# A graph-attention block on one core: for 6 of 16 source tiles ScalarE writes turned masks into the score banks, TensorE adds the scores; the first and the last stage are ordered anew

## The chip, the cores and the metric

The kernel runs on one core of one Trainium2 chip. The metric is the device time in microseconds (us) of one execution, the median of several. The engines are named PE (TensorE), DVE (VectorE), ACT (ScalarE), POOL (GpSimd) and SP (SyncE, which here only issues DMAs).

## The reference

One graph-attention layer with 2048 sources, 2048 targets, width 256, 8 heads of 32. Cut to what matters:

```python
h  = relu(layernorm(x));  hs = layer_norm(h) * s1 + b1;  ht = layer_norm(h_target) * s1 + b1
q, k, v = (ht @ Wq + bq) / sqrt(32), hs @ Wk + bk, hs @ Wv + bv
logits  = where(adj != 0, einsum('thd,shd->hts', q, k), -1e30)
ctx     = einsum('hts,shd->thd', softmax(logits), v)
ht      = layer_norm(ht + ctx @ Wo + bo) * s2 + b2
out     = x + ht + gelu(ht @ W1) @ W2
```

Everything is float32 in and out. The kernel splits most operands into a 16-bit high part and a 16-bit rest.

## The kernel before, in words

Targets are taken in 4 blocks (`NTB`) of 512, and in each block the 8 heads one after another: 32 *units* (`UNITS`), unit u being block k = u // 8 and head r = u % 8. A unit has 16 *steps* (`STEPS`), one for each tile of 128 sources; n = 16 u + step numbers them all, to 512.

A step n needs a tile of masked, shifted scores. `scores(n)` on PE writes it into one of two banks, `score[n % 2]`: four matmuls of 128 columns lay minus the mask, turned by the negative identity `nidentb` (`mask_nat` holds 1e30 where there is no edge, targets on the partitions), and one of 512 columns adds the scores. ACT takes the exponential into `prob` (`exponential(n)`), POOL or DVE makes its low part `prob_lo` (`low_part(n)`; DVE has steps 2, 6, 10 and 14 of most units), and `context(n)` on PE adds 8 matmuls of 65 columns to the bank `ctx`. PE issues `scores` five steps (`AHEAD`) before `context`; `scores(n)` waits for `exponential(n - 2)`, since the bank must be free.

The shift of a unit is the maximum of its scores, found ahead of time: `early_scores` (PE, 512 columns, two to a pair) and `maxima` (DVE, 1024 elements, with the mask) work on 8 pairs per unit, 14 pairs (`LEAD`) ahead, in two buffers `early`. So each pair on PE waits for the maxima of the pair two before. The maxima go through `shift_row` (PE), `negated` and `row_out` (ACT) into the query rows. One bank, `aux`, serves all small jobs one after another (`aux_job`, `AUX`): shift rows, turned contexts (`cT`), the output product (`wo`), turned targets (`qT`), query projections (`qp`). Tables such as `CT_AT` or `MASK_DVE` give (head, step) or (head, pair) of each; every engine runs its own list in order, with semaphores between them. ACT copies the context bank out once per unit (`context_out`), at the start of the next one.

The first stage normalizes, projects keys, queries and values, and moves keys and queries by DMA into the layout of the heads (`place_k`, `place_q`: 32 partitions x 1024 elements each, 48 + 12 of them, in groups g of two heads, all from SP). `sum_values` gives the mean of the values (for targets without an edge) by 32 matmuls into `aux`. `up_bias` in unit 1 computes the bias that the second layer norm's bias gives the feed-forward product, by 32 matmuls of one column, and `scale_weight` (DVE, units 2 to 5) multiplies W1 by the norm's scale.

The last stage runs the feed-forward part per block of targets: `up_products` (PE, 6 x 512 columns for each of 8 slices f), `gelus` (ACT, the function and a copy), `gelu_low` (DVE), `down_products`; between them `turn_block`, `block_high` and `block_low` bring in the next block, and `results` (DVE) frees the row banks.

## Time and profile before

| | |
|---|---|
| median of 3 runs (lowest, highest) | 723.34 us (723.26, 723.36) |
| profiled execution: its own time, its span | 727.01 us, 725.2 us |
| PE busy | 672.5 us (93%) |
| DVE busy | 591.6 us (82%) |
| POOL busy | 517.4 us (71%) |
| ACT busy | 451.7 us (62%) |
| first exponential starts, last context copy starts | 76.62 us, 620.76 us |

Busy is the time in which an engine runs at least one instruction, over the span. Matmuls overlap in the pipeline, so a busy PE is not one at its peak. The three stages are read apart: before 76.62 us, the 32 units up to 620.76 us, and the rest.

### The profile page before, as it was taken

The numbers are of one execution on the slowest core, as the hardware profiler recorded it, in microseconds if no ns is written. First come the engines' busy times: TensorE is split into PE (matmuls) and PEld (weight loads), VectorE is DVE, ScalarE is ACT, GpSimd is POOL, SyncE is SP. The second block draws the span as 40 slices with busy tenths as digits, with TensorE's granted clock in tenths as the row PEclk, the third lists the DMA queues.
The fourth block names the chain that finished last, engine by engine and source line by source line (L and its number), as shares of the span: only waits on it lengthen the run. The fifth ranks groups of instructions, "written<-read, shape, count | busy, mean of one in ns | idle before, by whom it ended". The sixth has DMA issues, their size and how long they took to land.

```text
span 725.2 us, 20296 instructions
## 1 busy us (share of the span) xinstructions
PE 672.5 (93%) x8386; PEld 479.8 (66%) x8386; DVE 591.6 (82%) x974; ACT 451.7 (62%) x806; POOL 517.4 (71%) x494
## 2 busy tenths in 40 slices
PE   4968889899999999999999999999999899889998
PEld 4536567666677677667767776677677667556667
DVE  5947687999989997999999899989977987554651
ACT  4632446666677656877766586677666778836650
POOL 3720657979899996789999778899977777442430
PEclk9979998999999999999999999999999999989999
DMA  8373610211200111130000201103000000000001
GB/s 296 112 196 79 236 31 2 70 45 57 81 2 2 31 57 34 44 104 17 2 31 2 89 30 54 38 2 118 2 2 2 3 2 2 1 1 23 23 22 52
DMA packets 20796, 36.22 MB, mean 50 GB/s; under 512 B 2752, under 2 KB 13280, under 8 KB 20704
## 3 DMA queue, kind: packets, MB, share of 16 engines
q1 hardware_dynamic: 20704, 34.92, 15.6%
q8 instruction: 66, 1.08, 0.6%
q14 instruction: 26, 0.21, 0.1%
HBM read 26.49 MB, written 2.10 MB: 39 GB/s over the span
## 4 chain that ended last, share of the span: by engine, by line
PE 56%; DVE 30%; issue 8%; SPq 2%; ACT 2%; DMA 1%; DVEq 0%; ACTq 0%
PE score L442 24%; DVE early L1147 14%; PE early L442 14%; PE ctx L442 10%; PE aux L442 6%; DVE prob_lo L1155 6%; SPq L358 2%; DVE mask_nat L1135 1%; DVE st_x L1070 1%; DVE half_max L1147 1%; DVE q_stage L1173 1%; DMA node_i<-in_nodemask 1%; DVE st_l L1065 1%; DMA kT<-mask_nat 1%; DVE col_l L1193 0%
## 5 line engine op out<-in xcount | busy, mean ns | idle before, releaser
L1350 POOL TENSOR_TENSOR prob_lo<-prob 128x512 f16<-128x512 f32 x376 | 434.9, 1181 | 109.8 <-ACT prob L856 108.3
L856 ACT ACTIVATE prob<-score 128x512 f32<-128x512 f32 x512 | 304.8, 597 | 173.9 <-PE score L442 166.2
L442 PE MATMUL early<-kT,qT 96*128 96x512 f16 x512 | 193.3, 383 | 28.1 <-DVE half_max L1147 20.8
L442 PE MATMUL score<-nidentb,mask_nat 128*128 128x128 bf16 x2048 | 198.9, 220 | 2.6 <-ACT prob L856 1.4
L442 PE MATMUL score<-qT,kT 97*128 97x512 f16 x512 | 196.0, 383 | 0.0
L442 PEld LDWEIGHTS ctx<-v_sb,prob 128*128 128x128 bf16 x2048 | 160.0, 98 | 54.3 <-ACT raw L878 9.3
L442 PE MATMUL ctx<-v_sb,prob 128*128 128x65 f16 x2048 | 192.3, 193 | 0.6 <-POOL prob_lo L1350 0.5
L442 PE MATMUL ctx<-v_sb,prob_lo 128*128 128x65 f16 x2048 | 191.1, 193 | 0.0
L1147 DVE CUSTOM_DVE_ANT_0 early<-early,mask_nat,half_max 128x1024 f32<-128x1024 f32 x128 | 163.6, 1285 | 28.4 <-PE early L442 27.9
L1147 DVE CUSTOM_DVE_ANT_0 early<-early,mask_nat 128x1024 f32<-128x1024 f32 x128 | 156.8, 1229 | 25.6 <-PE early L442 23.7
L442 PEld LDWEIGHTS ctx<-v_sb,prob_lo 128*128 128x128 f16 x2048 | 143.4, 97 | 50.2 <-issue 4.8
L1155 DVE TENSOR_TENSOR prob_lo<-prob 128x512 f16<-128x512 f32 x136 | 137.0, 1008 | 8.9 <-ACT prob L856 8.9
L442 PEld LDWEIGHTS score<-nidentb,mask_nat 128*128 128x128 bf16 x2048 | 122.4, 98 | 5.7 <-ACT prob L856 2.6
L442 PEld LDWEIGHTS early<-kT,qT 96*128 96x128 f16 x512 | 50.4, 99 | 49.3 <-DVE half_max L1147 40.0
L1449 POOL TENSOR_TENSOR mask_nat<-mask_nat,tgt 128x256 f32<-128x256 f32 x16 | 15.3, 966 | 51.7 <-DVE mask_nat L1300 51.7
L442 PEld LDWEIGHTS score<-qT,kT 97*128 97x128 f16 x512 | 50.2, 98 | 0.0
L1286 DVE TENSOR_TENSOR kT<-qT,kT 128x512 f16<-128x512 f32 x32 | 25.3, 794 | 26.8 <-ACT kT L1026 26.8
L442 PE MATMUL early<-w_f,kT 128*128 128x256 f16 x384 | 42.6, 273 | 1.6 <-DVE adj_in L1310 1.6
L442 PEld LDWEIGHTS early<-w_f,kT 128*128 128x128 f16 x384 | 37.5, 98 | 6.9 <-DVE adj_in L1310 1.9
L1021 ACT ACTIVATE qT<-score,bias_f 128x512 f32<-128x512 f32 x32 | 21.9, 684 | 28.2 <-PE score L442 24.8
L1147 DVE DVE_READ_ACCUMULATOR2_ANT half_max<- 128x1 f32 x256 | 35.4, 138 | 0.0
L1135 DVE TENSOR_SCALAR mask_nat<-adj_in 128x1024 bf16<-128x1024 int32 x26 | 29.6, 1140 | 0.0
(167 smaller groups left out, 609.1 us busy)
## 6 DMA issues: line engine op xcount, KB each, us to landing
adj_in<-in_adj SPq DMA_DIRECT2D x26, 512.0 KB, 3.8
qT<-q_stage SPq DMA_DIRECT2D x48, 64.0 KB, 2.0
kT<-mask_nat SPq DMA_DIRECT2D x48, 64.0 KB, 2.0
raw<-in_x SPq DMA_DIRECT2D x4, 512.0 KB, 5.1
tgt<-in_L_gnn_h_target SPq DMA_DIRECT2D x4, 512.0 KB, 8.4
prob<-in_adj SPq DMA_DIRECT2D x4, 512.0 KB, 8.4
nT<-in_L_gnn_W SPq DMA_DIRECT2D x2, 1024.0 KB, 7.5
mask_nat<-in_x SPq DMA_DIRECT2D x1, 2048.0 KB, 8.3
```

The costliest lines, as they stand in the source:

```text
L358: sp.dma_start(dst[r * HD:(r + 1) * HD, 2 * g:2 * g + 2, :].rearrange("p h t -> p (h t)"), stage[g * HD:(g + 1) * HD, part, :, :].rearrang ...
L442: return nc.tensor.matmul(dst, w, m, start=start, stop=stop, **more)
L856: nc.scalar.activation(prob[:, n % SLOTS, :], score[n % 2][:, :], ACT.Exp).then_inc(exp_done, 1)
L1021: nc.scalar.activation(gelu[:, f % 2, :], up[f % 2][:, :], ACT.Gelu_apprx_tanh, bias=bias_f[:, f:f + 1]).then_inc(gelu_ready, 1)
L1065: link(nc.vector.bn_stats(dst[:, n, :], tile))
L1070: last = nc.vector.bn_stats(dst[:, first + t, :], tile(t))
L1135: nc.vector.tensor_scalar(mask_half(k, i), adj_home(k, i), 0.0, BIG, ALU.is_equal, ALU.mult).then_inc(mask_dve, 1)
L1147: nc.vector.tensor_tensor_reduce(out=early[e % 2][:, :], in0=early[e % 2][:, :], in1=mask_nat[:, k % 2, t, half * HALF:(half + 1) * HALF], ...
L1155: nc.vector.tensor_tensor(prob_lo[:, n % SLOTS, :], prob[:, n % SLOTS, :], prob_hi(n % SLOTS), ALU.subtract).then_inc(lo_sem["dve"], 1)
L1286: nc.vector.tensor_tensor(g_lo[:, k % 2, f, :], gelu[:, f % 2, :], g_hi[:, k % 2, f, :], ALU.subtract).then_inc(g_lo_done, 1)
L1350: nc.gpsimd.tensor_tensor(prob_lo[:, n % SLOTS, :], prob[:, n % SLOTS, :], prob_hi(n % SLOTS), ALU.subtract).then_inc(lo_sem["pool"], 1)
L1449: nc.gpsimd.tensor_tensor(xin[:, n - 1, :], xin[:, n - 1, :], tgt[:, n - 1, :], ALU.add).then_inc(r_done, 1)
```

## The change

1. **Masks turned once a block.** For the source tiles in `TURNED` (6 of 16, in units 1 to 31) the four mask matmuls leave `scores`. `turn_masks` makes them once per block of targets in the bank `aux`, `masks_out` (ACT) copies them as bfloat16 into `mask_t`, and `preload(n)` (ACT) copies such a tile into the score bank; the one matmul of 512 columns adds to it. The preload stands two tiles ahead in ACT's list.
2. **Places.** Two masks, the context norms and sums, `CT_AT` and `WO_AT` move; in unit 0 all low parts are POOL's; the low weight parts get other units.
3. **First stage.** Four adjacency loads and one target load are issued before the first placements; every group has its own semaphore; groups 2 and 3 are placed after W1 is loaded, W2 is loaded in unit 8. The mean comes from sums of the features (`feature_sums`, DVE, 4 reductions of 1024 elements) and 2 matmuls.
4. **Norm 2.** `up_bias`, `bias_f` and `scale_weight` are gone. Instead `normed_high` is two ACT instructions (scale and bias into `h_full`, then the 16-bit copy), and `gelus` has no bias.
5. **Last stage.** Block 1 is turned after slice 2, its high part stands behind slice 4, its low part behind slice 5, ahead of the end of block 0's slices.

```diff
+TURNED = (2, 4, 6, 9, 11, 14)
+MT_AT = {(5, 12): 0, (6, 2): 1, (6, 12): 2, (7, 2): 3, (7, 5): 4, (7, 12): 5}
+MT_FIRST = {1: 0, 3: 1, 5: 2, 7: 3, 12: 4, 14: 5}
-MASK_DVE = [(0, 6), (2, 1), (2, 4), (2, 7), (3, 7), (4, 3), (4, 7), (5, 3)]
+MASK_DVE = [(0, 6), (2, 4), (2, 7), (3, 3), (3, 7), (4, 3), (4, 7), (5, 3)]
-SUM_AT = [(0, 3), (0, 11), (1, 1), (1, 7)]
-NORM_AT = [(0, 5), (1, 1), (1, 3), (1, 5)]
+SUM_AT = [(0, 3), (0, 11), (1, 3), (1, 11)]
+NORM_AT = [(0, 5), (1, 1), (1, 5), (2, 1)]
-DVE_LO = [(2, 6, 10, 14)] * (UNITS - 2) + [tuple(range(1, STEPS, 2))] * 2
+DVE_LO = [()] + [(2, 6, 10, 14)] * (UNITS - 3) + [tuple(range(1, STEPS, 2))] * 2
...
@@ SP
+                for i in range(TT, PAIRS):
+                    load_adj(0, i)
+                sp.dma_start(tgt[:, 3 * TT:4 * TT, :], rows(h_target, 3)).then_inc(tgt_in[3], 16)
                 staged(0)
                 place_q(0, range(1))
                 staged(1)
                 place_k(0, range(1))
-                for i in range(TT, PAIRS):
-                    load_adj(0, i)
-                place_q(0, range(1, TT))
+                place_q(0, range(1, 2))
...
@@ PE, scores
+                    elif is_turned(n):
+                        pe.wait_ge(preloaded, preloads(n))
                     else:
                         pe.wait_ge(exp_done, n - 1)
-                    for t in range(TT):
+                    for t in range(0 if is_turned(n) else TT):
...
-                def sum_values(g):
+                def mean_values():
+                    pe.wait_ge(feat_done, 1)
+                    pe.wait_ge(v_lo, NT // 2 - 1)
+                    for c in range(DC):
+                        last = mm(ctx[:, 0:D], feat_all[:, c:c + 1].to_broadcast([P, P]), wkv[:, 1, c, :], c == 0, c == DC - 1)
...
+                def turn_masks(k, i):
+                    m = TURNED[i]
+                    mask_ready(pe, k, m // PAIRS)
+                    aux_free(("mT", k, i))
+                    for t in range(TT):
+                        last = mm(aux[:, t * P:(t + 1) * P], mask_nat[:, k % 2, t, m * P:(m + 1) * P], nidentb[:, :], True, True)
...
@@ ACT
+                def preload(n):
+                    k, m = n // (H * STEPS), n % STEPS
+                    i = TURNED.index(m)
+                    act.wait_ge(exp_done, n - 1)
+                    act.wait_ge(aux_done, AUX["mT", k, i] + 1)
+                    nc.scalar.activation(score[n % 2][:, :], mask_t[k][:, i, :], ACT.Copy).then_inc(preloaded, 1)
...
                         if n + AHEAD < TILES:
                             exponential(n + AHEAD)
+                        if n + AHEAD + 2 < TILES and is_turned(n + AHEAD + 2):
+                            preload(n + AHEAD + 2)
...
-                    nc.scalar.activation(h_bufs[k % 2][:, 0, c, :], bank, ACT.Copy).then_inc(h_hi, 1)
...
+                    affine(h_full[:, c, :], bank, LN2_G[:, c:c + 1], LN2_B[:, c:c + 1]).then_inc(read, 1)
+                    act.wait_ge(read, count)
+                    nc.scalar.activation(h_bufs[k % 2][:, 0, c, :], h_full[:, c, :], ACT.Copy).then_inc(h_hi, 1)
...
                 for f in range(FC):
                     gelus(0, f)
+                    if f == 4:
+                        block_high(1)
                     if f in (5, 6):
                         context_T(NTB - 1, f - 5)
-                block_high(1)
...
@@ DVE
+                def feature_sums(c):
+                    dve.wait_ge(nT_masked, DC * (c + 1))
+                    return nc.vector.tensor_reduce(feat_sum[:, :, c], nT[:, c, :, :], AX, ALU.add)
...
                     if f < TT:
                         context_norm(NTB - 1, f)
-                block_low(1)
+                    if f == 5:
+                        block_low(1)
```

SP's queue in the first stage, before. `q_stage` and `mask_nat` are the staged queries and keys, `adj` the adjacency.

```order
L393 DMA tgt<-in_L_gnn_h_target 128x4x256 x2
L358 DMA qT<-q_stage 32x1024 x3
L358 DMA kT<-mask_nat 32x1024 x3
L353 DMA prob<-in_adj 128x1024 x2
L353 DMA prob_lo<-in_adj 128x1024 x2
L358 DMA qT<-q_stage 32x1024 x9
L358 DMA kT<-mask_nat 32x1024 x45
```

And the same place in the changed kernel:

```order
L408 DMA tgt<-in_L_gnn_h_target 128x4x256 x2
L368 DMA prob<-in_adj 128x1024 x2
L368 DMA prob_lo<-in_adj 128x1024 x2
L411 DMA tgt<-in_L_gnn_h_target 128x4x256
L373 DMA qT<-q_stage 32x1024 x3
L373 DMA kT<-mask_nat 32x1024 x3
L373 DMA qT<-q_stage 32x1024 x3
L373 DMA kT<-mask_nat 32x1024 x21
L431 DMA nT<-in_L_gnn_W 128x2x1024
```

The big loads now stand ahead of the first placements, and three query placements instead of nine stand between the first keys of block 0 and those of block 1.

ACT's list in unit 16 (block 2, head 0), before; `prob<-score` are the exponentials:

```order
L878 ACTIVATE raw<-ctx 128x4x65
L856 ACTIVATE prob<-score 128x512 x7
L868 ACTIVATE shift<-half_max 128x4
L856 ACTIVATE prob<-score 128x512 x3
L873 ACTIVATE qT<-aux 1x512
L856 ACTIVATE prob<-score 128x512 x6
```

The first two thirds of the same unit in the changed kernel; `score<-nT` are preloads (this block's turned masks lie in the space of `nT`), `w_f<-nT` is a part of W2:

```order
L909 ACTIVATE raw<-ctx 128x4x65
L879 ACTIVATE prob<-score 128x512 x3
L887 ACTIVATE score<-nT 128x512
L879 ACTIVATE prob<-score 128x512 x2
L887 ACTIVATE score<-nT 128x512
L879 ACTIVATE prob<-score 128x512 x2
L899 ACTIVATE shift<-half_max 128x4
L957 ACTIVATE w_f<-nT 128x512
L879 ACTIVATE prob<-score 128x512
L887 ACTIVATE score<-nT 128x512
L879 ACTIVATE prob<-score 128x512 x2
L904 ACTIVATE qT<-aux 1x512
```

A preload stands behind every second or third exponential.

ACT's list in the last stage, changed kernel, where before slice 5 followed slice 4 directly; `qT<-score` is the gelu, `kT<-qT` its copy, and `nT<-early,cols` with `qT<-nT` the two halves of `normed_high`:

```order
L1058 ACTIVATE qT<-score 128x512
L1062 ACTIVATE kT<-qT 128x512
L825 ACTIVATE nT<-early,cols 128x512
L968 ACTIVATE qT<-nT 128x512
L825 ACTIVATE nT<-early,cols 128x512
L968 ACTIVATE qT<-nT 128x512
L1058 ACTIVATE qT<-score 128x512
L1062 ACTIVATE kT<-qT 128x512
L928 ACTIVATE cT<-aux 128x512
```

Block 1's four instructions moved here from behind the last slice of block 0, where there were two.

## Rows read from the trace of the kernel before

**Rows 1.** Windows, one unit each: length, busy us by engine, PEclk, DMA share, GB/s
```profile
100.00:123.16 23.16, 21.80 (x265) 16.79 (x263) 15.33 (x23) 10.69 (x21) 14.70 (x15) 0.85 0.08 24
...
344.68:359.58 14.90, 14.90 (x233) 10.91 (x231) 13.53 (x21) 10.62 (x21) 14.90 (x14) 1.00 0.01 2
...
374.55:391.74 17.19, 15.50 (x233) 10.80 (x231) 17.19 (x25) 10.63 (x21) 17.19 (x17) 1.00 0.10 32
391.74:410.11 18.37, 18.37 (x257) 14.37 (x255) 17.08 (x25) 11.77 (x24) 16.68 (x16) 1.00 0.19 59
410.11:428.47 18.36, 18.36 (x257) 14.43 (x255) 15.17 (x27) 12.05 (x23) 13.70 (x13) 1.00 0.09 30
428.47:448.04 19.57, 18.72 (x241) 12.34 (x239) 17.84 (x30) 14.30 (x25) 13.44 (x13) 1.00 0.18 56
448.04:465.07 17.03, 15.56 (x233) 10.70 (x231) 17.03 (x23) 12.34 (x24) 15.74 (x14) 1.00 0.25 64
...
610.75:620.76 10.01, 9.24 (x182) 7.40 (x181) 6.97 (x7) 6.88 (x14) 7.15 (x6) 1.00 0.02 3
```

**Rows 2.** Groups by line in one unit, 344.68 to 359.58
```profile
L1350 POOL TENSOR_TENSOR prob_lo<-prob 128x512 f16<-128x512 f32 x13 | 15.3, 1209 | 0.0
L856 ACT ACTIVATE prob<-score 128x512 f32<-128x512 f32 x17 | 10.2, 597 | 4.6 <-PE score L442 4.4
...
L1147 DVE CUSTOM_DVE_ANT_0 early<-early,mask_nat,half_max 128x1024 f32<-128x1024 f32 x4 | 5.1, 1286 | 0.2 <-PE early L442 0.2
...
L1155 DVE TENSOR_TENSOR prob_lo<-prob 128x512 f16<-128x512 f32 x5 | 5.0, 995 | 0.0
L1147 DVE CUSTOM_DVE_ANT_0 early<-early,mask_nat 128x1024 f32<-128x1024 f32 x4 | 4.9, 1229 | 1.1 <-PE early L442 1.1
```

**Rows 3.** Timeline of PE, first stage
```profile
37.72 1.88 PE L442 MATMUL ctx<-nT,cT 128*128 128x512 f32 x4
...
49.54 1.01 PE L442 MATMUL early<-kT,qT 96*128 96x512 f16 x2 [6.50 <-DMA kT<-mask_nat]
50.35 3.62 PE L442 MATMUL ctx<-nT,cT 128*128 128x512 f32 x4
```

**Rows 4.** Windows of 4 us in the first stage, columns as in rows 1
```profile
28.00:32.00 4.00, 3.01 (x18) 2.42 (x17) 3.93 (x12) 3.35 (x6) 3.51 (x5) 1.00 0.02 4
...
48.00:52.00 4.00, 2.46 (x4) 1.14 (x5) 1.30 (x3) 0.00 (x0) 0.00 (x0) 0.50 0.46 115
```

**Rows 5.** Timeline of SP's queue, first stage
```profile
36.55 7.56 SPq L358 DMA_DIRECT2D qT<-q_stage  x9
44.21 34.58 SPq L358 DMA_DIRECT2D kT<-mask_nat  x45
```

**Rows 6.** Timeline of ACT, the first exponentials
```profile
76.62 1.08 ACT L856 ACTIVATE prob<-score 128x512 f32<-128x512 f32 x2 [0.71 <-PE score L442]
```

**Rows 7.** Timeline of PE, unit 1 (100.00 to 123.16)
```profile
103.81 4.16 PE L442 MATMUL aux<-cols,nT 128*128 128x1 f32 x32
...
108.24 0.62 PE L442 MATMUL score<-nidentb,mask_nat 128*128 128x128 bf16 x4
...
109.96 0.62 PE L442 MATMUL score<-nidentb,mask_nat 128*128 128x128 bf16 x4
...
117.31 0.39 PE L442 MATMUL score<-nidentb,mask_nat 128*128 128x128 bf16 x4
117.54 0.38 PE L442 MATMUL score<-qT,kT 97*128 97x512 f16 x1
```

**Rows 8.** Timeline of PE, last stage
```profile
636.73 5.30 PE L442 MATMUL score<-qT,w_f 128*128 128x512 f16 x12 [3.37 <-DVE qT L1199]
...
663.99 5.41 PE L442 MATMUL early<-w_f,kT 128*128 128x256 f16 x48 [1.59 <-DVE adj_in L1310]
```

**Rows 9.** Groups by line over the whole span
```profile
L1026 ACT ACTIVATE kT<-qT 128x512 f16<-128x512 f32 x32 | 20.2, 630 | 1.0
...
L802 ACT ACTIVATE nT<-score,cols 128x512 f32<-128x512 f32 x8 | 5.7, 769 | 0.0
```

More of the change, by code:

```diff
@@ L107, in aux_numbers @@
 def aux_numbers():
-    jobs = [("mean", 0), ("mean", 1), ("shift", 0)] + [aux_job(u, s) for u in range(UNITS) for s in range(STEPS) if aux_job(u, s)]
+    jobs = [("shift", 0)] + [aux_job(u, s) for u in range(UNITS) for s in range(STEPS) if aux_job(u, s)]
     jobs += [("cT", NTB - 1, c) for c in range(DC)] + [("wo", NTB - 1, i) for i in range(TT // 2)]
@@ L144, in lo_here, with is_turned, preloads @@
     return [n for n in [*first, *soon] if n < TILES and LO_DONE[n][0] == "dve"]
+def is_turned(n):
+    return n >= STEPS and n % STEPS in TURNED
+def preloads(n):
+    return sum(is_turned(i) for i in range(n + 1))
 def adj_use(k, i):
@@ L334, in masks_free @@
                 for c in range(NTB):
-                    eng.wait_ge(k_first[c], FIRST)
-                    eng.wait_ge(k_placed[c], REST)
+                    for g in range(TT):
+                        eng.wait_ge(k_placed[c][g], PLACE)
             else:
@@ L630, in turn_normed @@
                     return last
-                def up_bias():
-                    pe.wait_ge(w_in[0], 16)
-                    aux_free(("bf", 0))
-                    for f in range(FC):
-                        for c in range(DC):
-                            last = mm(aux[:, f:f + 1], w1[:, c, f * P:(f + 1) * P], LN2_B[:, c:c + 1], c == 0, c == DC - 1)
-                    last.then_inc(aux_ready, 1)
                 pe.wait_ge(made, 3)
@@ L964, in _ @@
                     high_values(i)
-                act.wait_ge(q_first, FIRST)
-                act.wait_ge(q_placed[0], REST)
-                for g in range(2):
-                    mean_out(g)
+                mean_high()
                 negated(0)
```

210 lines of the change are left out of this document (103 added, 107 removed).

## The prediction

> **What bounds the kernel now.** I read the page first: PE 93% busy, but that is an average over three stages. Then windows of one unit each, cut where ScalarE starts its copy of the context bank (32 such copies). Three kinds of unit show in [rows 1]. In 344.68 to 359.58 PE is busy all 14.90 us (0.93 a step), but so is POOL, and DVE 13.53: PE leads by little. In 391.74 to 410.11 and 410.11 to 428.47 PE is full for 18.4 us (float32 turns and products through `aux`) while DVE and POOL have 1.3 to 4.7 us of room: PE alone bounds. In 374.55 to 391.74 and 448.04 to 465.07 DVE is full and PE has 1.5 us of room: there a faster PE buys nothing. By kind and count: 9 heavy units (4, 10, 11, 12, 18, 19, 20, 26, 27), 8 where DVE or POOL is full or nearly (2, 3, 5, 9, 13, 17, 21, 25), 11 plain ones, the last two (30, 31), and units 0 and 1 by themselves.
>
> Then the places where PE stands still. In the first stage it waits 6.50 us for a placement of keys, and the four products behind it take 3.62 us where the same four took 1.88 before [rows 3]; the granted clock there is 0.50, the 1.2 GHz level, after PE had done almost nothing [rows 4]. SP explains the wait: nine query placements take 7.56 us ahead of the keys of block 1, at 0.77 each later on (34.58 over 45) [rows 5]. The 2 MB of adjacency issued just ahead of them share the DMA engines, which had been idle at 28 to 32 (share 0.02, [rows 4]). In unit 1 the 32 one-column matmuls take 4.43 us until the next score (103.81 to 108.24), and the steps behind them 1.72 us each (108.24 to 109.96) [rows 7]: unit 1 is 23.16 us long [rows 1]. In the last stage PE waits 3.37 us for block 1's low part, and the 12 products behind it take 5.30 us [rows 8]; 12 x 512 columns at the pace of the 48 x 256 ones (5.41 us for twice the columns) are 2.7.
>
> **The change part by part.**
>
> *Unit 1.* `up_bias` goes: 4.43 us, and about three steps of 1.72 instead of 0.91: 2.4. Together **-6.9 us**. The clock's part hangs on what PE does before it: the rows show full clock up to the one-column matmuls and the lower level behind them. The Trainium skill, "TensorE: Matmul & The Clock Gate", section "HAM oscillation — how this bites in real kernels", says that a PE left idle comes back at half rate; the trace agrees after the two idle waits, and here also after busy but narrow matmuls.
>
> *First stage.* The four adjacency loads and the target load (2.5 MB) go into the hole at 24 to 31 us; three query placements instead of nine stand before block 1's keys. SP is through with the adjacency at 36.55 [rows 5], so it would be ready near 34.5 without it; three queries and three keys at 0.77 end at 39.1 and land 2 to 3 us later. PE is ready at 43.04 (49.54 less 6.50, [rows 3]): the 6.50 us wait goes, and with it the slow products (1.7 us, and an estimated 0.9 for the four on the other bank): -9.1. ScalarE no longer copies two means ahead of the shift: -0.8. Against this DVE gets four reductions of 1024 elements. The trace shows none; the nearest row is the maxima of 1024 elements, 1.23 us [rows 2]; bounds 0.6 (half of it, if a reduction without a second input were twice as fast) to 1.3. I take 1.23, 4.9 in all, of which I hide 1.5 in holes where DVE waits for the last projection; DVE is full otherwise, so 3.4 shows. Sum **-6.5**; the first exponential starts at 70 instead of 76.62 [rows 6]. SP then still places groups 2 and 3 (30 placements of 0.77, to about 85) and only then loads the next adjacency; DVE wants it at about 91. If that slips, up to 4 us come back.
>
> *Unit 0.* Four low parts leave DVE, which paces this unit with 14 pairs; **-1.5**. POOL makes all 16, in about 17 us, with room.
>
> *Masks in units 2 to 31.* Four mask matmuls cost PE 0.23 us (117.31 to 117.54, [rows 7]); six tiles are 1.4 us per unit, about 42 us in 30 units. The turns give back 24 x 0.23 = 5.5 us, 4 of it here. What passes through:
> - Heavy units: 18.4 becomes 17.0 for PE; DVE at 17.08 to 17.84 ends last in two of three [rows 1]. I take 1.1 each, **-10**.
> - DVE-bound units: nothing from PE. A norm of head 1 and a mask of head 2 move to where DVE has room, `scale_weight` leaves four units (0.9 each, estimated from twice a 512-element pass): **-5** over eight units.
> - Plain units: POOL needs 12 x 1.21 = 14.5 [rows 2], DVE eight maxima at 1.23 to 1.29, their reads, and four low parts at 1.0, about 14.2. So 14.9 can fall to 14.5 at best: 0.3 each, **-3.3**.
> - The last two have no maxima; PE loses 2.8, but ScalarE gets nine to twelve preloads: **-1.5**.
>
> *What ScalarE pays.* 186 preloads and 24 copies. The preload reads SBUF and writes PSUM, which no row shows; bounds are the exponential, 0.597 [rows 2], and the SBUF copy, 0.630 [rows 9]. Two exponentials back to back end 1.08 us after the first began [rows 6], so one more costs 0.49 when ScalarE doesn't wait. A plain unit's 10.62 us [rows 1] become 13.6 to 14.4, below 14.9 but no longer far. By the Trainium skill, "ScalarE: Activation LUTs", section "Step-by-step: what each stage is for", a write to PSUM is faster than one to SBUF; that would put the preload at the lower bound, and no row here shows it. The chain: `scores(n)` now waits for exponential(n-2) and a preload, some 1.1 to 1.2 us after the score is there, and PE comes back to it after two steps, 1.7. Slack about 0.3; each other job of ScalarE (context copy, shift row, mask copies) that falls between eats it. PE waits 0.1 to 0.3 us for some of them, and mostly has that time. Heads 5 to 7 also carry the mask copies, and head 4 (14.30 before) goes to 17.8 of 19.57. I take **+5** over the 30 units; bounds 0 and +20 (0.1 for each preload).
>
> *Last stage.* Block 1's low part stands behind slice 5, so the 3.37 us wait and the slow products (2.6) go. But ScalarE now spends (0.77 + 0.63) x 2 on a block [rows 9] instead of two copies, ahead of slice 5, and PE waits for that: net -4.7. For block 2 the same extra 1.7 us stands on the chain to `results`, where PE already waits 1.59 [rows 8]; for block 3, about 0.8. If the longer wait brings the lower clock, 2.6 more. I take +3.2: **-1.5**. Gelus without bias hide under PE's six products.
>
> **Sum** against the profiled execution's span of 725.2: -6.5 - 1.5 - 6.9 - 10 - 5 - 3.3 - 1.5 + 5 - 1.5 = -31.2. The medians lie 2 us below the span; I carry the difference over: 723.3 - 31.2 = **692 us**.
>
> **Rivals.**
> - *Units gain nothing* (15%): POOL, DVE and ScalarE together hold every unit at its old length. For it: three engines above 90% in plain units, with buffers of two. Against it: PE alone is full in nine units. Then only -6.5 - 1.5 - 6.9 - 1.5: 707 us.
> - *PE's cut passes in full* (8%): if DVE's and POOL's lengths are mostly contention that eases. Then -38 for units 2 to 31: 669 us. Against it: DVE full at 17.19 and 17.03 [rows 1].
> - *ScalarE becomes the bound, slower* (5%): PE stands at each preloaded tile. The gains outside the masks are 16.4 us. If preloads lengthen a unit beyond its old length by more than 0.55 us (0.09 for each of 186), all is lost; at 0.2 us, 37 us, it is 744. For it: the slack of 0.3 us and head 4. Against it: ScalarE idles 4.6 us of a plain unit waiting for scores [rows 2].
>
> **How the numbers follow.** My forecast has 72%, its own range 680 to 703 from the bounds (preload penalty 0 to +15, first stage -4 to -9, last stage +1 to -5). The range that should hold 8 in 10 reaches towards the first rival: 679 to 707. A measurement tells 0.2% (1.4 us) from no change. Faster: 0.94; within: 0.01; slower: 0.05.
>
> **What would show it.** Right: no wait for `kT<-mask_nat` on PE and clock 1.00 through 40 to 60 us; the first exponential near 70; unit 1 near 16; heavy units near 17.3; plain units 14.4 to 14.9; preloads at 0.6; ScalarE busy about 82%; last stage near 103 us. Wrong: heavy units still 18.4, or PE waiting for ScalarE's preloads by tens of microseconds in the table of waits; plain units above 15.5; DVE waiting for adjacency in unit 0.

## The result

The changed kernel takes 734.1 us (median of 4 runs, 732.1 to 737.1) against 723.4 (4 runs, 723.3 to 723.7): ratio 1.015, interval 1.011 to 1.019. It is slower, and the forecast was 692.0.

The profiled execution took 735.73 us, its span is 733.5 (725.2 before). The execution that was profiled of the kernel before took 727.01 us, 3.6 above the median of its runs, so differences against it in profiled executions come out 2 to 3 us more favourable to a kernel than medians do. The page of the changed kernel, busy time by engine and the line of the preloads:

```profile
PE 653.0 (89%) x7678; PEld 445.7 (61%) x7678; DVE 584.6 (80%) x972; ACT 559.1 (76%) x1021; POOL 511.4 (70%) x495
...
L887 ACT ACTIVATE score<-nT 128x512 f32<-128x512 bf16 x138 | 83.0, 602 | 4.4
```

The first stage went as forecast. These are timelines of the changed kernel, PE and then ScalarE (start, us, instruction, idle before it and what ended it):

```profile
43.40 0.60 PE L466 MATMUL early<-kT,qT 96*128 96x512 f16 x2
43.83 1.88 PE L466 MATMUL ctx<-nT,cT 128*128 128x512 f32 x4
```

```profile
69.54 1.08 ACT L879 ACTIVATE prob<-score 128x512 f32<-128x512 f32 x2 [0.71 <-PE score L466]
```

The wait of 6.50 us and the slow products behind it [rows 3] are gone, and the first exponential starts at 69.54 instead of 76.62 [rows 6]. Unit 1 takes 14.67 us instead of 23.16.

From unit 2 on the time is given back. Windows of single units of the changed kernel, columns as in rows 1; in order they are units 2, 18, 19, 20, 22, 24, 29 and 30:

```profile
110.74:131.46 20.72, 15.82 (x206) 10.37 (x205) 18.66 (x22) 13.67 (x27) 14.97 (x16) 0.92 0.08 27
384.89:407.76 22.87, 19.93 (x230) 13.84 (x230) 17.28 (x27) 15.59 (x31) 19.25 (x19) 0.93 0.07 25
407.76:426.76 19.00, 17.70 (x229) 13.08 (x229) 14.89 (x30) 15.73 (x31) 13.66 (x14) 1.00 0.18 57
426.76:446.60 19.84, 17.83 (x214) 11.31 (x213) 18.82 (x28) 17.49 (x32) 15.02 (x13) 1.00 0.17 54
463.34:478.90 15.56, 14.66 (x213) 10.18 (x213) 12.61 (x21) 14.37 (x29) 13.04 (x13) 1.00 0.01 3
494.53:509.19 14.66, 14.23 (x205) 9.89 (x205) 13.23 (x22) 13.52 (x27) 14.27 (x15) 1.00 0.11 36
583.98:602.97 18.99, 16.43 (x214) 10.86 (x213) 15.06 (x23) 17.60 (x34) 13.00 (x13) 1.00 0.01 2
602.97:617.36 14.39, 12.03 (x193) 8.82 (x192) 10.19 (x15) 13.48 (x26) 9.28 (x9) 1.00 0.01 2
```

Unit 18 took 18.37 us before [rows 1] and takes 22.87; the plain unit 22 takes 15.56, above the 14.90 of [rows 1], though PE is busy for less in it. ScalarE is busy 14.37 of those 15.56 us, where it had 10.62 of 14.90 [rows 1].

The units by kind, in us, measured in the profiled executions between the starts of ScalarE's context copies. "no_turned" is the changed kernel without its turned masks, "none_tables" has five tables of places of before as well (both below): the third number column is what the turned masks do, the last what the rest of the change does with those places left alone.

| stretch | forecast | changed - before | changed - no_turned | none_tables - before |
|---|---|---|---|---|
| to the end of unit 1 | -14.9 | -12.4 | +0.9 | -11.9 |
| 9 heavy units | -10 | +11.6 | +3.2 | -0.2 |
| units 3, 5, 9, 13, 17, 21, 25 | -5, unit 2 included | -4.2 | -0.4 | -1.2 |
| unit 2 | | +4.9 | +5.2 | 0.0 |
| 11 plain units | -3.3 | +5.2 | +6.3 | -1.1 |
| last two | -1.5 | +2.1 | +2.1 | 0.0 |
| last stage | -1.5 | +1.2 | -0.1 | -1.8 |
| ScalarE's pay, inside the rows above | +5 | | | |
| sum | -31.2 | +8.3 | +17.2 | -16.2 |

### The profile page after: what moved, and what is told of

Its sections match the earlier page's. It is cut to its first block and busy times, and to the rows that moved or that the text cites. A ratio compares the mean times of both kernels' runs of the same rounds, so it can differ in the third digit from the quotient of the medians.

```text
span 733.5 us, 19341 instructions
## 1 busy us (share of the span) xinstructions
PE 653.0 (89%) x7678; PEld 445.7 (61%) x7678; DVE 584.6 (80%) x972; ACT 559.1 (76%) x1021; POOL 511.4 (70%) x495
## 5 line engine op out<-in xcount | busy, mean ns | idle before, releaser
L1398 POOL TENSOR_TENSOR prob_lo<-prob 128x512 f16<-128x512 f32 x380 | 426.7, 1144 | 126.9 <-ACT prob L879 125.6
L879 ACT ACTIVATE prob<-score 128x512 f32<-128x512 f32 x512 | 298.2, 592 | 77.4 <-PE score L466 72.1
L466 PE MATMUL early<-kT,qT 96*128 96x512 f16 x512 | 194.4, 385 | 16.8 <-DVE half_max L1188 16.2
L466 PE MATMUL score<-qT,kT 97*128 97x512 f16 x512 | 199.2, 389 | 10.6 <-ACT score L887 10.2
L466 PE MATMUL ctx<-v_sb,prob 128*128 128x65 f16 x2048 | 193.7, 194 | 16.2 <-ACT raw L909 16.1
L466 PEld LDWEIGHTS ctx<-v_sb,prob 128*128 128x128 bf16 x2048 | 160.5, 98 | 74.3 <-ACT raw L909 30.1
L1196 DVE TENSOR_TENSOR prob_lo<-prob 128x512 f16<-128x512 f32 x132 | 127.4, 965 | 8.5 <-ACT prob L879 8.5
L466 PE MATMUL score<-nidentb,mask_nat 128*128 128x128 bf16 x1304 | 128.2, 221 | 4.0 <-ACT prob L879 1.7
L887 ACT ACTIVATE score<-nT 128x512 f32<-128x512 bf16 x138 | 83.0, 602 | 4.4
L466 PEld LDWEIGHTS score<-nidentb,mask_nat 128*128 128x128 bf16 x1304 | 78.3, 98 | 9.7 <-ACT prob L879 6.3
L466 PE MATMUL early<-w_f,kT 128*128 128x256 f16 x384 | 44.4, 279 | 3.7 <-DVE adj_in L1357 3.7
L1333 DVE TENSOR_TENSOR kT<-qT,kT 128x512 f16<-128x512 f32 x32 | 28.0, 881 | 21.5 <-ACT kT L1062 21.5
L1058 ACT ACTIVATE qT<-score 128x512 f32<-128x512 f32 x32 | 19.0, 594 | 26.4 <-PE score L466 23.1
```

The lines of the kernel that those rows point to most:

```text
L466: return nc.tensor.matmul(dst, w, m, start=start, stop=stop, **more)
L879: nc.scalar.activation(prob[:, n % SLOTS, :], score[n % 2][:, :], ACT.Exp).then_inc(exp_done, 1)
L887: nc.scalar.activation(score[n % 2][:, :], mask_t[k][:, i, :], ACT.Copy).then_inc(preloaded, 1)
L1058: nc.scalar.activation(gelu[:, f % 2, :], up[f % 2][:, :], ACT.Gelu_apprx_tanh).then_inc(gelu_ready, 1)
L1196: nc.vector.tensor_tensor(prob_lo[:, n % SLOTS, :], prob[:, n % SLOTS, :], prob_hi(n % SLOTS), ALU.subtract).then_inc(lo_sem["dve"], 1)
L1333: nc.vector.tensor_tensor(g_lo[:, k % 2, f, :], gelu[:, f % 2, :], g_hi[:, k % 2, f, :], ALU.subtract).then_inc(g_lo_done, 1)
```

## The experiments

Each time is compared with runs of the kernel before on the same chip (their medians were 723.4 to 724.0 us); edits are against the changed kernel unless said otherwise.

### Masks off, half of them, or turned and not used

```diff
 # no_turned
-MT_AT = {(5, 12): 0, (6, 2): 1, ...}
-MT_FIRST = {1: 0, 3: 1, 5: 2, 7: 3, 12: 4, 14: 5}
+MT_AT = {}
+MT_FIRST = {}
 def is_turned(n):
-    return n >= STEPS and n % STEPS in TURNED
+    return False
 #   (and W2's load waits for the exponentials of block 0, not for its preloads)
 # turned3
-TURNED = (2, 4, 6, 9, 11, 14)
+TURNED = (4, 9, 14)
+MT_AT = {(6, 2): 0, (7, 2): 1, (7, 12): 2}
+MT_FIRST = {3: 0, 7: 1, 14: 2}
 # copies_only: is_turned(n) returns False, MT_AT and MT_FIRST stay
```

Expected of no_turned: 

> The changed kernel with no tile turned: TensorE adds all masks to the scores again, with no turning of masks, no copies of them and no preloads; all else as in the changed kernel (first stage, tables, last stage). Theory, the turned masks cost more on ScalarE than they save on TensorE: ScalarE was busy 14.7 of 15.6 us in the plain units in which it also copies turned masks; they return from 15.6 to 14.9 us (six of them, 4.0 us), units 28 to 30 from 18.8, 19.0 and 14.4 to about 17.9, 17.2 and 12.8 (4.2 us), while the units without copies lose 0.3 to 0.5 us each (some 12 of them, 5 us): 731 us (728 to 734). If the late norm is independent of the masks, units 18 and 26 stay above 21 us here too. Rival, the steps of the record: the masks save TensorE 0.7 to 1.1 us per unit after all and other parts of the change cost more; then this kernel takes 745 to 755 us.

Measured: 717.3 us, 0.990 of before (0.988 to 0.992). The rival, the steps on record, is out by some 30 us; the theory had the sign and was itself low: 17 us, not 3. The six plain units with copies are back at 14.9, units 28 to 30 at 17.9, 17.1 and 12.9, as it said. Units 10, 18 and 26 stayed at 21.1, 20.5 and 23.6.

Expected of turned3: 

> The changed kernel with 3 source tiles of 16 turned (4, 9 and 14) instead of 6, and so 3 mask copies a block and 3 preloads a unit. Theory, ScalarE is near its bound and every preload and copy beyond its room costs time: with half the load the plain units come to 14.6 to 14.9 us whether or not they hold a mask copy, units 29 and 30 lose about half of what they gained (18.1 and 13.6 us), and the time is below both the changed kernel and the one with no tile turned: 727 us (724 to 731). Rival, the cost is per preload and not a bound (each waits in turn with the exponentials): the time is midway between 734 and that of the kernel with none, within 1.5 us. Rival of the record, masks on ScalarE pay: slower than the changed kernel by some 5 us.

Measured: 720.2 us, 0.993 (0.991 to 0.995). That is below the theory's range, and still above none (717.3), where the theory had it below; the rivals' times are out. Three tiles cost 3 us over none, six cost 17: the cost is steeply more than proportional. Plain units without copies took 14.5 to 14.6 (unit 16: 14.60, all of it PE).

Expected of copies_only: 

> The changed kernel with the masks still turned on TensorE and copied by ScalarE, but never used: TensorE adds all masks to the scores as before, and no bank is preloaded. It stands between the kernel with no tile turned (717.3 us) and the changed one (734.1) and splits the 16.8 us between them. Theory, the preloads are the cost: units 28 to 31, which hold preloads and no copies, were 4.7 us longer in the changed kernel, and the long VectorE low part of unit 2 came only with six preloads; the copies cost 24 narrow matmuls and some 4 us of ScalarE a block: 722 us (719 to 726). Rival, turning and copying is the cost, through VectorE's and TensorE's wait for the aux bank in units 0, 6, 7, 14, 15, 22, 23: 728 to 732, with the plain units at 15.6 us here as well.

Measured: 722.5 us (718.7 to 725.4), 0.998 (0.996 to 1.000). Turning and copying costs some 5 us, the preloads some 12. The theory's time is met, but so is one mark of the rival: the six plain units that hold copies take 15.4 to 15.6 us without any preload (3.4 us together). There PE is full: units 6 and 7 took 15.36 and 15.57 us, all of them PE, 0.47 and 0.67 above no_turned, and two and three turns at 0.23 us [rows 7] are 0.46 and 0.69. Of the preloads' 12 us, 4.8 lie in units 28 to 31 and 5.2 in unit 2 alone (see there).

### ScalarE relieved

```diff
 # half_exp; half_exp_none is this and no_turned together
-nc.scalar.activation(prob[:, n % SLOTS, :], score[n % 2][:, :], ACT.Exp)
+nc.scalar.activation(prob[:, n % SLOTS, 0:TB // 2], score[n % 2][:, 0:TB // 2], ACT.Exp)
```

Expected of half_exp: 

> The changed kernel with every exponential on 256 of the 512 columns of its tile (the other half of the probabilities is left stale; all other work stays). It takes about 0.2 us off each of 512 ScalarE instructions of 0.6 us. Theory, ScalarE is what makes the turned masks dear: relieved of some 3 us a unit, the units with mask copies fall from 15.6 us to below 14.6, units 29 and 30 from 19.0 and 14.4 to about 17.0 and 12.5, and the gap of 16.8 us to the kernel with no tile turned shrinks to between -8 and +4: 707 to 718 us. Rival, the cost lies in handing the bank from engine to engine and in TensorE's turning, and not in ScalarE's load: the gap stays over 10 us.

Expected of half_exp_none: 

> The kernel with no tile turned, with the same exponentials on 256 of 512 columns (half of the probabilities stale). It is what the kernel before is to be compared with. Theory: TensorE and VectorE bound its units, so the relief of ScalarE brings 0 to 4 us: 713 to 717 us, with the plain units at 14.9. Rival, ScalarE was part of its bound too: under 712.

Measured: 706.9 us with six tiles turned (706.4 to 707.6), 0.977 of before (0.974 to 0.979), and 710.5 with none (709.9 to 716.3), 0.983 (0.980 to 0.987): the order is reversed, as the theory had it. The second came out below its range, at its rival: the kernel with no tile turned gains 6.9 us too, so ScalarE was part of its bound as well. In the profiled executions the masks added 17.3 us up to the last context copy with whole exponentials, and take off 1.1 with halves; the last stage's clock adds 1.6 to that. Windows of unit 16 with six turned tiles, then with none, both with half exponentials:

```profile
339.04:353.11 14.07, 13.72 (x206) 9.56 (x205) 13.64 (x22) 10.72 (x28) 14.07 (x14) 1.00 0.01 3
```

```profile
342.06:356.87 14.81, 14.81 (x233) 10.91 (x231) 13.96 (x23) 7.63 (x20) 14.35 (x15) 1.00 0.01 3
```

PE's cut is real: 14.81 us, all of it PE, become 14.07, where POOL is full. With whole exponentials units 8, 16 and 24 gave 0.7 us together; with 3 us more of room on ScalarE two of the three give 0.7 each. The six plain units with copies go from 4.3 us lost to 0.9 gained. But the gain is small even then: over the nine heavy units it is 2.0 us against the 10 of the forecast, 1.3 of it in head 4, 0.9 in head 3, and none in head 2, where both kernels have the late norm of the next section. In unit 20, of head 4 (19.20 us), VectorE is busy 18.99:

```profile
409.22:428.42 19.20, 17.89 (x215) 11.24 (x214) 18.99 (x30) 14.10 (x32) 14.46 (x13) 1.00 0.18 56
```

Yet unit 12 took 19.21 us with VectorE at 17.42, so a full VectorE isn't shown to be what holds head 4.

The halves do not tell ScalarE's load from its order. They also shorten the chain of every step (an exponential takes 379 ns instead of 592), and what does not shrink with them stays: PE's weight loads wait 22.0 us for the copies of the context bank (30.1 with whole exponentials, 9.8 with halves and no turned masks), and units 28 to 31 keep 2.4 us of their 4.8. In unit 28 of the changed kernel ScalarE's timeline shows why; below it is PE's:

```profile
566.94 1.28 ACT L937 ACT_TABLE_LOAD   x1
568.24 0.30 ACT L937 ACTIVATE col_l<-mv_l,big 128x4 f32<-128x4 f32 x1
568.55 1.28 ACT L879 ACT_TABLE_LOAD   x1
569.85 0.60 ACT L879 ACTIVATE prob<-score 128x512 f32<-128x512 f32 x1
570.48 0.60 ACT L887 ACTIVATE score<-nT 128x512 f32<-128x512 bf16 x1
```

```profile
571.13 0.39 PE L466 MATMUL score<-qT,kT 97*128 97x512 f16 x1 [1.82 <-ACT score L887]
```

In head 4 of every later block (units 12, 20 and 28) ScalarE changes its function table for one small root and back, 1.28 us each time, as in the kernel before. The exponential and the preload behind the two loads come late, PE waits 1.82 us for the preload, and the granted clock of the unit is 0.91. With half exponentials this wait is still 1.52 and the clock 0.91; with no tile turned PE waits 0.97 us there for the exponential, and the unit takes 17.85 us instead of 18.75. This part is order, not load.

### The late context norm

In the changed kernel PE stands at the first turn of the context in units 10, 18 and 26. This is unit 26, PE's timeline and then VectorE's:

```profile
530.69 0.72 PE L619 MATMUL aux<-ident,q_stage 128*128 128x128 f32 x4 [2.39 <-DVE q_stage L1215]
```

```profile
529.59 1.05 DVE L1215 TENSOR_TENSOR q_stage<-raw,rden 128x256 f32<-128x256 f32 x1
533.30 1.23 DVE L1188 CUSTOM_DVE_ANT_0 early<-early,mask_nat 128x1024 f32<-128x1024 f32 x1 [2.67 <-PE early L466]
```

The fourth norm, which `NORM_AT` moved to (2,1), starts when PE has stood there for 1.3 us (530.69 less 2.39 is 528.30), and VectorE then idles 2.67 us for the early scores that stand behind the turn on PE. From 530.70 to 534.00 the granted clock was 0.57.

```diff
 # norm_early; none_norm is this and no_turned together
-SUM_AT = [(0, 3), (0, 11), (1, 3), (1, 11)]
-NORM_AT = [(0, 5), (1, 1), (1, 5), (2, 1)]
+SUM_AT = [(0, 3), (0, 11), (1, 1), (1, 7)]
+NORM_AT = [(0, 5), (1, 1), (1, 3), (1, 5)]
 # none_ct6: no_turned, and
-CT_AT = {(2, 4): 0, (2, 10): 1}
+CT_AT = {(2, 6): 0, (2, 10): 1}
 # none_tables: none_norm, and CT_AT, WO_AT, MASK_DVE, LOAD_AT as before
```

Expected of norm_early: 

> The changed kernel with the third and fourth context sum and norm at their places of before (sums at (1,1) and (1,7), norms at (1,3) and (1,5)) and the turns of the context still at (2,4) and (2,10). Theory, the fourth norm is late: in units 10, 18 and 26 TensorE waited 1.8, 2.0 and 2.4 us for the norm that the change had moved to (2,1), and ran at half clock after it; with the norm seven pairs earlier these waits are under 0.3 us, units 18 and 26 are back from 22.9 and 23.3 to about 18 us, unit 10 from 20.8 to about 19, and the time is 734.1 - 10 = 724 us (722 to 727). Rival, ScalarE is what makes those units long (it also writes two turned contexts there): they stay above 21 us and the time is 731 to 735.

Measured: 728.6 us, 1.005 (1.003 to 1.007). Units 10, 18 and 26 fell to 18.9, 19.3 and 19.6 (9.3 us together), but units 9, 17 and 25 grew by 2.4, and the first stage with units 0 and 2, where the two kernels don't differ, came out 1.9 longer: a little over half of the gain passes to the total, which is above the theory's range. The three waits for the norm are gone, as the theory said; unit 10 came out as expected, units 18 and 26 1.3 and 1.6 us above. None stayed above 21 us, so ScalarE, the rival, is not what made them long.

Expected of none_norm: 

> The changed kernel with no tile turned and with the third and fourth context sum and norm at their places of before: two of the experiments together. In the one with no tile turned, units 10, 18 and 26 still took 21.1, 20.5 and 23.6 us. Theory, the late norm and the masks are two independent losses: these three come to about 19, 18.5 and 19 us, and the time is 717.3 - 8.5 = 709 us (707 to 712), below both kernels. Rival, without the preloads the early norm takes VectorE's room in units 9, 17 and 25 (one was 1.1 us longer with it): 712 to 716.

Measured: 712.8 us, 0.985 (0.983 to 0.987). Late norm and masks are about independent losses: the early norm gains 4.4 us without masks and 5.5 with them. The time is the rival's (712 to 716) and not the theory's 709, for units 9, 17 and 25 took 17.2, 17.9 and 16.3.

Expected of none_ct6: 

> No tile turned, sums and norms as in the changed kernel (the fourth norm at (2,1)), and the first turn of the context two tiles later, at (2,6) instead of (2,4). Theory, units 10, 18 and 26 pay for TensorE's wait of 1.8 to 2.4 us at that turn and for the half clock behind it; two tiles are 1.9 us, so nearly all of the wait goes, and units 9, 17 and 25 keep what the late norm gives them (16.5, 16.8 and 15.6 us; with the early norm 17.2, 17.9 and 16.3): 709 us (707 to 712), below the kernel with the early norm (712.8). Rival, the turn then collides with the shift row at step 8 or the second turn at 10, and TensorE waits for the aux bank there: 712 to 716.

Measured: 711.8 us, 0.985 (0.982 to 0.987). That is at the end of the theory's range, but two tiles later helps in part only: 20.2, 21.3 and 20.5 us, and 3.1 of the 6.3 us between the profiled executions are the last stage's clock. Unit 26 still has a wait for the norm, 0.8 us; unit 18 none, but PE waits there for GpSimd's low parts. In GpSimd's list the late context sum and a low part of W2 stand ahead of them; which of the two delays them was not tested. This is from the table of waits of none_ct6, unit 18 (what waits, for what: us, times, longest):

```profile
PEld ctx L466 <- POOL prob_lo L1398: 2.8, 3, 1.3
```

Expected of none_tables: 

> No tile turned, and all five tables of places as in the kernel before: context sums, norms, turns of the context, rows of Wo, VectorE's masks and adjacency loads. What is left of the change is the new first stage, the late W2, the scaling of the rows in place of the weights, and the last stage. Theory, the moved places of head 2 explain units 10, 18 and 26: they are within 0.5 us of the kernel before (19.3, 18.4, 18.9), and the time is 723.4 - 13.3 (up to the end of unit 1) - 0.4 (unit 2) + 1.2 (last stage) = 711 us (709 to 713), which is no better than with either half of the tables, since units 9, 17 and 25 are back at 17.2, 17.2 and 16.3. Rival, the places that remain moved (turns at (2,4) and (2,10)) cost by themselves: 707 to 709.

Measured: 710.7 us, 0.981 (0.979 to 0.983). With the five tables as before the three units took 19.33, 18.38 and 18.90, those of before to 0.01 us: all that they had lost was the moved places. Units 9 and 25 are back too; unit 17 stays 0.7 longer (17.90 against 17.19), and the low parts of W2, which the change moved to units 17 to 20, were not put back; whether they are the cause was not tested.

### Six or three tiles on clean ground

```diff
 # six_tables: all tables as before, TURNED as changed, and for unit 2
-DVE_LO = [()] + [(2, 6, 10, 14)] * (UNITS - 3) + ...
+DVE_LO = [(), (2, 6, 10, 14), tuple(range(1, STEPS, 2))] + [(2, 6, 10, 14)] * (UNITS - 5) + ...
 # three_tables: TURNED = (4, 9, 14), MT_AT = {(5, 12): 0, (6, 12): 1, (7, 5): 2},
 #   tables as before, and no tile turned in the last block:
+    return STEPS <= n < (NTB - 1) * H * STEPS and n % STEPS in TURNED
```

Expected of six_tables: 

> Six tiles turned as in the changed kernel, with all tables of places as in the kernel before and unit 2's low parts shared eight and eight. Theory, ScalarE's load is the cost of the masks, and the late norm and the blocked VectorE were losses of their own: it stands above the kernel with no tile turned and the same tables by 5 (turning and copies) + 5 (last block) + 1 to 2 = 10 to 12 us: 722 us (719 to 725), level with the kernel before. Rival, most of the 16.8 us came from the masks' clash with the late norm and the backlog: within 5 us of the other, 712 to 716.

Measured: 724.2 us, 1.001 (0.999 to 1.003), as the theory had it, 13.5 above none_tables; the profiled executions are 11.6 apart. 4.8 of these lie in units 28 to 31, which have preloads and no copies, 4.3 in the six plain units with copies, 2.0 in the heavy ones, 1.7 in unit 0 and 1.6 in unit 2, against gains of 1.8 in unit 1 and 0.7 in units 8, 16 and 24. The tables of waits of six_tables, then of none_tables:

```profile
ACT prob L879 <- PE score L466: 62.3, 126, 1.6
PEld ctx L466 <- ACT raw L909: 28.6, 30, 1.4
PE ctx L466 <- ACT raw L909: 15.0, 29, 0.9
PEld score L466 <- ACT score L887: 14.6, 31, 1.9
PE score L466 <- ACT score L887: 10.5, 23, 1.8
```

```profile
ACT prob L879 <- PE score L466: 157.8, 344, 2.0
...
PEld ctx L466 <- ACT raw L909: 9.2, 30, 0.5
```

Without turned masks ScalarE waits for PE 344 times: it is up to date in two steps of three, and PE's wait for its copy of the context bank is 0.3 us a unit, the copy itself. With them it waits 126 times, and PE waits for ScalarE: 28.6 us instead of 9.2 at the context bank, whose copy stands in ScalarE's program behind exponentials and preloads, and 14.6 us for preloads.

The same units of none_tables, to be set beside units 22, 29 and 30 of the changed kernel above; PE, ScalarE and the length tell it:

```profile
450.77:465.67 14.90, 14.90 (x233) 10.92 (x231) 13.18 (x22) 10.62 (x20) 13.32 (x12) 1.00 0.01 2
...
566.42:583.56 17.14, 16.24 (x241) 11.73 (x239) 14.95 (x23) 14.38 (x28) 13.02 (x12) 1.00 0.01 2
583.56:596.41 12.85, 12.47 (x222) 9.81 (x219) 11.21 (x16) 10.53 (x20) 9.70 (x8) 1.00 0.01 3
```

In unit 30 ScalarE goes from 10.53 of 12.85 us to 13.48 of 14.39, in unit 29 from 14.38 of 17.14 to 17.60 of 18.99.

The kernel t3_norm_three is turned3 with the norms of norm_early and, like three_tables, no tile turned in the last block.

Expected of t3_norm_three: 

> Three tiles turned (4, 9, 14), and only in the first three blocks of queries, with sums and norms at their places of before. The kernel with three turned tiles took 720.2 us with the late norm, and its units 28 to 31 were 2.4 us longer than those with no tile turned. Theory: 720.2 - 8.5 (norm) - 2.4 (last block) - 1 (no copies in block 2): 708.5 us, level with the kernel with no tile turned and early norms, within 2 us; the units without mask copies are 0.3 us shorter than there (14.6 for 14.9), those with two copies 0.2 longer. Rival, three preloads cost as in proportion to six: 715 or more.

Measured: 712.2 us, 0.983 (0.982 to 0.985); none_norm, its like without masks, 712.8: level, as expected, though 3.7 us above the expected time, since none_norm was itself higher than foreseen.

Expected of three_tables: 

> Three tiles turned in the first three blocks of queries, their copies one to a unit in heads 5, 6 and 7, all tables of places as in the kernel before. Theory, TensorE gains 0.3 us in the units where it is the bound (some 10 of 24), and ScalarE's copies cost it in units 0 and 7: within 1.5 us of the kernel with no tile turned and the same tables. Rival, a small dose pays: faster than that one by 2 to 4 us.

Measured: 711.8 us, 0.984 (0.982 to 0.987), against 710.7 for none_tables: level again. A dose that ScalarE can carry does not pay either: 0.1 to 0.4 us off six of the plain units, and 0.7 more in each of units 3, 12 and 20. Unit 22 of three_tables, which holds preloads and no copies:

```profile
453.79:468.28 14.49, 14.49 (x221) 10.41 (x219) 12.63 (x21) 12.11 (x24) 13.53 (x13) 1.00 0.01 3
```

ScalarE is busy 12.11 of 14.49 us, and PE is full again. But without the mask matmuls of three tiles PE's unit is only 0.41 us shorter than 14.90, 0.14 for a tile, where the forecast took 0.23 from [rows 7].

### Unit 2

The changed kernel's VectorE, then its GpSimd, in unit 2:

```profile
116.86 6.14 DVE L1196 TENSOR_TENSOR prob_lo<-prob 128x512 f16<-128x512 f32 x1
122.92 1.22 DVE L1188 CUSTOM_DVE_ANT_0 early<-early,mask_nat 128x1024 f32<-128x1024 f32 x1
```

```profile
113.38 1.08 POOL L1402 TENSOR_SCALAR tgt<-tgt,col_t 128x256 f32<-128x256 f32 x1
114.43 8.02 POOL L1398 TENSOR_TENSOR prob_lo<-prob 128x512 f16<-128x512 f32 x8
```

A low part that takes VectorE 0.7 us took 6.14; it stood while GpSimd worked off the last six of its eight (1.00 us each, to 122.45). PE then waited 4.5 us for the maxima, and the granted clock of the unit fell to 0.92.

```diff
 # lo_unit0
-DVE_LO = [()] + [(2, 6, 10, 14)] * (UNITS - 3) + ...
+DVE_LO = [(2, 6, 10, 14)] * (UNITS - 2) + ...
 # lo_unit2: the DVE_LO of six_tables above
```

Expected of lo_unit0: 

> The changed kernel (734.1 us) with the low parts of tiles 2, 6, 10 and 14 of unit 0 given back to VectorE; the change had left all 16 of them to GpSimd. Theory, a backlog on GpSimd: in unit 2 GpSimd ran eight low parts back to back (8.02 us from 114.43), and VectorE's own low part, which started at 116.86 and took 6.14 us instead of 0.70, ended only when they did; with four fewer on GpSimd in unit 0 there is no such run in unit 2, no VectorE low part is over 1.7 us, and unit 2 is back from 20.7 us to about 16: 729 us, and the times scatter less than the 732.1 to 737.1 of the changed kernel. Rival one: the 6.14 us are an accident of one execution; then the time stays within 1 us of 734. Rival two: VectorE has no room for the four in unit 0 (its maxima start at 74.4 us), unit 0 and 1 are longer by 1 to 3 us, and the time is 731 to 736.

Measured: 735.5 us, 1.013 (1.010 to 1.017): a miss for my theory, and not for rival one either, since the trace holds the same instruction again, 6.13 us at 118.30 beside 8.02 us of GpSimd. The time is in rival two's range, but units 0 and 1 are not longer (26.59 and 14.67 us, against 26.53 and 14.67). It is no accident, and GpSimd's share of unit 0 is not its cause. By the timeline the backlog builds up over the four target rows that GpSimd scales between low parts from 108 to 114.5 us; that is only argued from the rows.

Expected of lo_unit2: 

> The changed kernel with VectorE making eight low parts in unit 2 instead of four, and GpSimd eight instead of twelve beside its target rows. In the changed kernel and in both kernels with other tables but six turned tiles, unit 2 holds one VectorE low part of 6.13 to 6.14 us, which ends with a run of eight GpSimd low parts back to back; with 3 turned tiles and a run of 12 none was over 1.6. Theory, GpSimd's backlog keeps VectorE from reading until it is worked off: with four fewer on GpSimd it never runs more than three back to back, no VectorE low part is over 1.7 us, unit 2 takes 15.5 to 16.5 us instead of 20.7, and the time is 734.1 - 4.5 = 729.5 us. Rival one, VectorE's own load is the bound of unit 2: it stays over 18 us with no long low part in it. Rival two, the long low part is bound to the mask preloads on ScalarE: it is still there, and the time is 734.

Measured: 731.3 us, 1.011 (1.009 to 1.013). Unit 2 takes 15.98 (4.7 less; unit 10 came out 1.6 longer), as expected, and the time is 1.8 us above the expected one; the longest VectorE low part there is 1.53, and GpSimd is no longer in arrears:

```profile
116.28 1.34 POOL L1398 TENSOR_TENSOR prob_lo<-prob 128x512 f16<-128x512 f32 x1 [0.47 <-ACT prob L879]
118.02 1.35 POOL L1398 TENSOR_TENSOR prob_lo<-prob 128x512 f16<-128x512 f32 x1 [0.40 <-ACT prob L879]
119.82 1.29 POOL L1398 TENSOR_TENSOR prob_lo<-prob 128x512 f16<-128x512 f32 x1 [0.46 <-ACT prob L879]
```

By the Trainium skill, "SBUF — State Buffer", section "SBUF: two separate sides", a VectorE instruction with two inputs from SBUF and a GpSimd instruction that reads SBUF share a pair of ports as an exclusive lock, held by one of them for a whole instruction. The trace agrees that VectorE stands, but for six instructions of GpSimd in a row and not one. A backlog alone isn't enough: with three tiles turned GpSimd ran 17 back to back in 19.83 us, 1.17 each, and VectorE's low parts came in between them at 1.2 to 1.5. Nor are six tiles: with half exponentials (half_exp) unit 2 took 15.38 us, against 15.50 with none turned, behind a longer backlog. Its GpSimd, and VectorE's low part of the same time:

```profile
113.18 19.69 POOL L1398 TENSOR_TENSOR prob_lo<-prob 128x512 f16<-128x512 f32 x17
```

```profile
115.36 1.40 DVE L1196 TENSOR_TENSOR prob_lo<-prob 128x512 f16<-128x512 f32 x1
```

What decides between the two is open.

### The last stage

```diff
 # none_norm_block: none_norm, and block 2's rows (block_high(1)) behind the loop
-                    if f == 4:
-                        block_high(1)
                     if f in (5, 6):
                         context_T(NTB - 1, f - 5)
+                block_high(1)
```

Expected of none_norm_block: 

> The kernel with no tile turned and early norms (712.8 us), with ScalarE's high parts of the second block's rows at their place of before, behind the seventh gelu and the last two context turns. In the last stage of the changed kernel TensorE waited 2.7 us for one of these turns, where the kernel before waited 0.3, and the stage took 105.6 us instead of 104.4. Theory: the wait goes and the stage takes 103 to 104.5 us: 711 us (710 to 712). Rival, the high parts are late in their turn for the next up product, as in the kernel before where TensorE waited 3.4 us for that block's low parts: no gain within 0.7 us.

Measured: 717.6 us, 0.991 (0.989 to 0.993), so 4.7 slower than none_norm (3.6 in the last stage of the profiled executions). The wait of 2.7 went, and PE waits 4.7 us for the second block's low parts instead: the rival, and worse than it said. The changed kernel has the better order.

What was left of this stage's loss is the clock. PE in the changed kernel, then in none_tables, at the same place:

```profile
640.95 1.09 PE L619 MATMUL aux<-ident,q_stage 128*128 128x128 f32 x4 [2.67 <-ACT cT L928]
```

```profile
619.46 0.63 PE L619 MATMUL aux<-ident,q_stage 128*128 128x128 f32 x4 [2.66 <-ACT cT L928]
```

The wait is the same, but in one execution the lower clock follows it (1.09 us for the same four) and in the other it does not. The stage takes 105.4 to 105.7 us, 104.1 to 104.2, or 102.6 in the profiled executions of kernels whose code of this stage is the same. From 640.95 to 645.00 the granted clock is 0.65 in the changed kernel; over the whole stage of none_tables it is 1.00.

## Why the prediction was wrong

**What held.** The first stage (first exponential at 69.54, forecast 70), the wait for the placed keys, the full clock there, and unit 1 (14.67, forecast near 16). For unit 1 that is 16.42 without turned masks; the other 1.8 us are the masks', which the forecast had not counted in this unit. Unit 0 did not get its 1.5 us: it grew by 3.2 (26.53 against 23.38), and 2.6 of that came with the turned masks (its end is at 96.07, and at 93.46 in no_turned). Around the first shift VectorE idles 6.65 us, up to 74.40, where before it idled 4.78; the forecast counted neither. Up to the end of unit 1: -12.4, forecast -14.9. The last stage was forecast at 103; it is 102.6 at full clock and 105.6 in the profiled execution.

**The step that failed first: "Masks in units 2 to 31" with "What ScalarE pays".** The forecast was -10 and -3.3 and -1.5 for the gain and +5 for the pay, net -9.8; taken out of the changed kernel the turned masks prove to cost 17.2 us, and 11.6 to 13.5 on clean ground. The sizes on ScalarE were right (preload 602 ns, ScalarE 14.37 us in a unit with copies, forecast 13.6 to 14.4). The reading was wrong: I took "below 14.9" for room. ScalarE must be idle when a bank is ready, since PE waits for its copy of the context and for its preloads; at 10.62 of 14.90 us it was in two steps of three, with six preloads (13.5 to 14.4 us of ScalarE) it is late. The half exponentials show that ScalarE's time turned a small gain into a loss in the plain units with copies and the heavy ones; whether through its load or through the length of each step's chain they do not tell apart. They leave half of the loss in the last block, where the order behind the table loads is part of it. The turning of the masks, priced at 5.5 us, held: copies_only came out 5.2 above none, 0.5 to 0.7 us in a plain unit with copies. I had the mechanism as the third rival, at 5%, with the point from which it decides: 0.09 us for each of 186 preloads. Copies_only gives the preloads 11.6 us, 0.062 each, and 5.2 of these are unit 2, another mechanism. That the whole of the masks, 17.2 us, comes to 0.092 a preload is luck.

**The gain itself was also too large.** The heavy units were to give 1.1 us each. With ScalarE relieved they gave 2.0 over nine. One reason is the price of the mask matmuls, 1.4 us for six tiles: the plain unit that PE filled gave 0.41 for three. What else holds the heavy units at their length is open; in head 4 VectorE was busy 18.99 of 19.20 us in one unit and 17.42 of 19.21 in another.

**The second step: "A norm of head 1 and a mask of head 2 move to where DVE has room".** I costed the move on VectorE alone and did not ask who reads the norm. The first turn of the context on PE does, two tiles behind it. Units 10, 18 and 26 rose by 10.4 us in sum, 9.3 of which went with the norm's old place. The seven VectorE-bound units did give 4.2, of which 1.2 are left with the old places.

**Unit 2**, 4.9 us, stood in no step: a VectorE low part stood behind GpSimd's backlog. It came only with six turned tiles and whole exponentials, and lo_unit2 takes it out.

**What remains of the change.** Without turned masks and with the old tables (none_tables) it gains 12.8 us by medians and 16.2 in the profiled executions: 11.9 of these up to the end of unit 1, 1.8 in the last stage, 2.5 between. That kernel, at 710.7, beats both. Why VectorE was let in between GpSimd's instructions in some kernels, and the lower clock after equal waits in some executions, stays open.

## What to carry to other kernels

An engine's idle time is not room if another engine waits for its answers: look at how often it waits for work (344 times here, or 126) beside its busy share, and expect the cost to start before 100% (unit 22 grew by 0.7 us with ScalarE at 14.37 of 15.56, and did not at 12.11 of 14.49). Look too at what stands ahead of each answer in its list. When an instruction is moved in its engine's list, ask who reads its result and when. A cut on one engine paid little here in stretches where a second engine was nearly full, so count those stretches by windows before pricing the cut.

## What the runs showed of the hardware

- One VectorE instruction with two SBUF inputs stood for 6.13 to 6.14 us behind six GpSimd instructions, at nearly the same length in three kernels. In another, with 17 such instructions back to back in 19.69 us, it stood for no more than 1.52.
- After the same wait of PE, 2.66 and 2.67 us, the granted clock fell in one execution and not in another; that alone is up to 3 us in a stage of 103.
- ScalarE loaded a function table in 1.28 us, twice in each head 4 of a later block.
- ScalarE's 128x512 pass takes 602 ns from SBUF (bf16) to PSUM, 585 from PSUM to SBUF as bf16, and 630 from SBUF to SBUF as float16 (the last in [rows 9] too).
